# GpSimd makes o + 1 for both halves of an LSTM step, in place of ScalarE for the second half

## The chip, the cores and the metric

One core of one Trainium2 chip runs the whole program. The metric is the device time of one execution in microseconds (us); the figure for a kernel is the median of its runs. The engines are TensorE (PE; its weight loads are listed apart as PEld), VectorE (DVE), ScalarE (ACT), GpSimd (POOL) and SyncE (SP). Each runs its own list of instructions in order, and they wait for one another on semaphores.

## What is computed

Two layers with residuals over x of shape (8, 512, 512): batch 8, 512 time steps, width 512.

```python
def lstm_scan(x, h0, Wx, Wh, b):
    xW = jnp.einsum('ntd,dg->ntg', x, Wx) + b
    def step(carry, xw_t):
        prev_h, prev_c = carry
        a = xw_t + prev_h @ Wh
        i = sigmoid(a[:, :Hdim]);  f = sigmoid(a[:, Hdim:2*Hdim])
        o = sigmoid(a[:, 2*Hdim:3*Hdim]);  g = tanh(a[:, 3*Hdim:])
        next_c = f * prev_c + i * g
        next_h = o * jnp.tanh(next_c)
        return (next_h, next_c), next_h
x = x + lstm(x, cond, Wx, Wh, b)
x = x + ssm(x, cond, ...)   # a per-step filter, projections, a linear scan of 64 states, a projection
```

The LSTM's 512 steps depend on one another. The second layer follows block by block, 32 steps at a time, beside the steps of the first.

## The kernel before, in words

**Halves.** The 512 hidden units lie in four chunks of 128 partitions; half 0 of a step is chunks 0 and 1, half 1 is chunks 2 and 3. Each half has its own PSUM bank (recA, recB), its own buffers (`tr`, `pre`, `act`, `prod`, `tc`, `osc`, index 0 or 1) and its own semaphores. The recurrent product is made in fp16 with the weights as a high and a low part (`whi`, `wlo`) and the state as a high and a low part (`hb`), so the state of a half is ready only when both its parts are written.

**One step, engine by engine.** TensorE, `recur(t, half, k)` at L465, multiplies chunk k of the old state into one half's bank: 8 matmuls a call, in the order A0, A1, B0, A2, A3, B1, B2, B3 (letter: the bank; digit: k). A0 waits for both parts of the state's half 0 (`s_h[0]`), A2 for those of half 1 (`s_h[1]`). VectorE: `open_` (L812, transposes a bank to SBUF), `add` (L818, sums the high and low columns to `pre`), `product` (L823), `cell` (L828, the new c), `high` (L834, high part of h = osc * tc) and `low` (L840, low part, from GpSimd's h less the high part). ScalarE: `gates` (L699, one tanh for all four gates), `seeds` (L626, puts the next step's x part into a bank, ahead of time), `tanh_c` (L709, tc = tanh of c) and `opened` (L705). The sigmoids are made from tanh, so h needs (o + 1), scaled by SC = 4096; that is `osc`. `gates` puts the tanh of o in `act[q][:, 2, :]`; `osc[0]` is made from it by GpSimd (L400, a tensor_scalar on 128x16), `osc[1]` by ScalarE (L705). GpSimd then makes h = osc * tc in fp32 for each half (L406).

**What sets the order.** All of it is written out by hand, and an engine never leaves its order. ScalarE in step t:

```python
gates(t, 0); seeds(t + 1, 0); gates(t, 1); tanh_c(t, 0)
opened(t);   seeds(t + 1, 1); tanh_c(t, 1)
```

VectorE in step t: `open_(0), add(0), open_(1), product(0), add(1), cell(0), product(1), high(0), cell(1), low(0), high(1), low(1)`, and after every fourth step `output` (L849, adds h to the residual). GpSimd in step t: osc of half 0, h of half 0, h of half 1. Once a step's own instructions are issued, each of TensorE, ScalarE and VectorE does its `beside(t)`: a share of the projection of later x (L435), of the second layer's filter (L510), its softplus, scan and outputs, put on certain steps by planned costs (`post_at`, `project_at`). These jobs stand in the same queues as the steps.

Of the kernel before, what the change touches and what calls it, by code (L numbers as in the profile page):

```python
# [5 lines left out]
def lstm_ssm_kernel(nc: bass.Bass, x, cond, Wx, Wh, b, conv_b, Wp, bp, Ws, bs, A_log, dt_log, Wo, bo, out):  # L6
# [5 lines left out]
    ALU = mybir.AluOpType  # L12
    ACT = mybir.ActivationFunctionType
# [12 lines left out]
    SC = 4096.0  # L26
# [5 lines left out]
    with ctx:  # L32
        def sb(name, shape, dt=f32):
            return ctx.enter_context(nc.sbuf_tensor(name, shape, dt))
# [4 lines left out]
        def sem(name):  # L39
            return ctx.enter_context(nc.semaphore(name))  # L40
# [32 lines left out]
        scale = sb("scale", [128, 4])  # L73
        tr = [sb(f"tr{h}", [128, 2, G, 4, NB]) for h in range(2)]
        pre = [sb(f"pre{h}", [128, G, 2, NB]) for h in range(2)]
        act = [sb(f"act{h}", [128, G + 1, 2 * NB]) for h in range(2)]
        prod = [sb(f"prod{h}", [128, 2, 2 * NB]) for h in range(2)]
        tc = [sb(f"tc{h}", [128, 2 * NB]) for h in range(2)]
        osc = [sb(f"osc{h}", [128, 2 * NB]) for h in range(2)]
# [33 lines left out]
        s_os = [sem(f"s_os{q}") for q in range(2)]  # L113
# [22 lines left out]
        s_tg = [sem(f"s_tg{q}") for q in range(2)]  # L136
# [243 lines left out]
        @block.gpsimd  # L380
        def _(pool):
            pool.memset(ident[:, :], 0.0).then_inc(s_zero, 1)
            pool.wait_ge(s_zero, 1)
            pool.affine_select(out=ident[:, :], in_=ident[:, :], compare_op=ALU.not_equal, fill=1.0, base=0,
                               pattern=[[-1, 128]], channel_multiplier=1).then_inc(s_ident, 1)
            pool.memset(bhl[:, :].bitcast(f32), 0.0).then_inc(s_bz, 1)

            pool.wait_ge(s_bhi, 2)
            pool.tensor_tensor(bhl[32:33, :], brow[1], bhl[32:33, :].bitcast(f32), ALU.subtract).then_inc(s_bl, 1)
            for k in range(2, KC):  # L390

                if k == 2:
                    pool.wait_ge(s_bl, 1)
                else:
                    pool.wait_ge(s_wxl_p, k - 2)
                pool.wait_ge(s_wxh_a, k - 1)
                pool.tensor_tensor(wxl[:, k, :], rawx[k], wxh[:, k, :].bitcast(f32), ALU.subtract).then_inc(s_wxl_p, 1)
            for t in range(T):
                pool.wait_ge(s_tg[0], t + 1)
                pool.tensor_scalar(osc[0][:, :], act[0][:, 2, :], 1.0, SC, ALU.add, ALU.mult).then_inc(s_os[0], 1)  # L400
                for q in range(2):
                    pool.wait_ge(s_tc[q], t + 1)
                    pool.wait_ge(s_os[q], t + 1)
                    if t % HS == 0 and t and q == 0:
                        pool.wait_ge(s_yadd, t // HS)
                    pool.tensor_tensor(h32[:, 2 * q:2 * q + 2, t % HS, :],  # L406
                                       osc[q][:, :].rearrange("p (c b) -> p c b", c=2),
                                       tc[q][:, :].rearrange("p (c b) -> p c b", c=2), ALU.mult).then_inc(s_h32[q], 1)
# [183 lines left out]
        def _(act_eng):  # L592
# [29 lines left out]
            def seeds(t, q):  # L622

                if t % TS == 0 and q == 0:
                    act_eng.wait_ge(s_seedin[t // TS % 2], 256 * (t // TT + 1))
                act_eng.activation(rec[q][:, 0:256], seed[:, t // TS % 2, t % TS // 2, q, :],  # L626
                                   ACT.Copy, scale=mask[:, t % 2:t % 2 + 1]).then_inc(s_seed[q], 1)
# [50 lines left out]
            def beside(t):  # L678
                for i in range(NP):
                    order = post_order(i)  # L680
                    for j in range(len(order)):
                        if post_at[i][j] == t:
                            post(i, order[j])
                for j in due(t, *PAR, len(par_order)):
                    param(j)
                for n in range(NBLK):
                    for i in range(2):
                        if out_when[n, i][2] == t:
                            o_store(n, i)
                for g in range(2, NG):  # L690
                    for part in range(2):
                        if ev_when(g) + part == t:
                            x_evacuate(g, part)
                for g, c in tiles_done(t):
                    x_rows(g, c)

            def gates(t, q):
                act_eng.wait_ge(s_add[q], t + 1)
                act_eng.activation(act[q][:, 0:G, :].rearrange("p g n -> p (g n)"),  # L699
                                   pre[q][:, :, :, :].rearrange("p g c b -> p (g c b)"), ACT.Tanh, scale=gain).then_inc(s_tg[q], 1)  # L700

            def opened(t):

                act_eng.wait_ge(s_tg[1], t + 1)
                act_eng.activation(osc[1][:, :], act[1][:, 2, :], ACT.Copy, bias=SC, scale=SC).then_inc(s_os[1], 1)  # L705

            def tanh_c(t, q):
                act_eng.wait_ge(s_c[q], t + 2)
                act_eng.activation(tc[q][:, :], act[q][:, 4, :], ACT.Tanh, scale=0.5).then_inc(s_tc[q], 1)  # L709
# [44 lines left out]
            for t in range(END):  # L754
                if t < T:
                    gates(t, 0)
                    if t + 1 < T:
                        seeds(t + 1, 0)
                    gates(t, 1)
                    tanh_c(t, 0)  # L760
                    opened(t)
                    if t + 1 < T:
                        seeds(t + 1, 1)
                    tanh_c(t, 1)
                beside(t)
# [318 lines left out]
```

## Time and profile before

| | |
|---|---|
| median of 3 runs | 1992.09 us (1990.87 to 1992.61) |
| the profiled execution's own time | 1992.87 us |
| its span, first to last instruction | 1991.0 us |
| mean granted TensorE clock | 0.987 of full |
| busy: PE, PEld | 1791.8 us (90%), 1282.6 us (64%) |
| busy: VectorE | 1430.1 us (72%) |
| busy: ScalarE | 1043.9 us (52%) |
| busy: GpSimd | 349.4 us (18%) |
| steps run from / to | about 78 us to 1972 us |

Busy shares say how full an engine is, not which one sets the time: 512 steps hang on each other, and in each the work goes from engine to engine. Matmuls overlap, and their ends are modelled, so TensorE's busy time is not a measure of how near it is to its limit. Read the chain of waits and a single step first. Where a duration and a start are given below, the end is their sum; a start earlier than the previous end on the same engine means that the two overlap in the engine.

### The profile page before, as it was taken

The page shows a single profiled execution, that of the slowest core. Times are in us where ns is not written, and L with a number is a line of the kernel's source. Part 1 is how long each engine was busy: PE and PEld are TensorE (multiplying, and loading weights), DVE is VectorE, ACT ScalarE, POOL GpSimd, SP SyncE. Part 2 cuts the span into 40 slices and gives each one's busy share as a digit, 9 for nine tenths or more (in the row PEclk, how much of TensorE's full clock was granted, in tenths as well). Part 3 has the DMA queues.
Part 4 walks back from the last instruction along what each step waited for, and adds up shares of the span by engine and source line. Part 5 has one row for each costly group of instructions (what it writes and reads, how often), then busy time and mean ns, then how long its engine had stood idle before and what let it go on. Part 6 is the DMA issues. An engine that isn't in the chain of part 4 may idle for free.

```text
span 1991.0 us, 90455 instructions
## 1 busy us (share of the span) xinstructions
PE 1791.8 (90%) x36290; PEld 1282.6 (64%) x36290; DVE 1430.1 (72%) x6913; ACT 1043.9 (52%) x4056; POOL 349.4 (18%) x1546
## 2 busy tenths in 40 slices
PE   2688899999999999999999999999999999999976
PEld 1455666666666666666666666766666677666755
DVE  4577666777777777777767777777777777767775
ACT  3355555555555555555555555555555555555452
POOL 3011111111111111111111111111111111111110
PEclk8799999999999999999999999999999999999998
DMA  5111111111121111111111111111111111211100
GB/s 201 49 47 44 39 50 36 40 55 48 37 61 49 42 45 51 49 41 58 46 48 46 44 46 51 53 49 49 46 39 51 50 52 34 66 45 40 47 17 23
DMA packets 112284, 98.71 MB, mean 50 GB/s; under 512 B 20097, under 2 KB 86197, under 8 KB 110838
## 3 DMA queue, kind: packets, MB, share of 16 engines
q1 hardware_dynamic: 111490, 92.35, 15.3%
q8 instruction: 286, 4.69, 1.0%
q14 instruction: 134, 1.10, 0.2%
q10 hardware_dynamic: 374, 0.57, 0.1%
HBM read 50.90 MB, written 41.94 MB: 47 GB/s over the span
## 4 chain that ended last, share of the span: by engine, by line
PE 45%; DVE 33%; ACT 11%; issue 5%; POOL 4%; DMA 1%; SPq 0%; ACTq 0%; POOLq 0%; DVEq 0%
PE recA L465 25%; DVE tr L812 16%; PE recB L465 9%; DVE pre L818 7%; ACT act L699 5%; PE pw L435 5%; PE pbc L510 5%; POOL h L406 4%; DVE hb L840 3%; ACT tc L709 3%; DVE prod L823 2%; DMA xs<-in_L_cond_b_dram 1%; ACT recB L626 1%; DVE acc L893 1%; DVE st L914 0%
## 5 line engine op out<-in xcount | busy, mean ns | idle before, releaser
L699 ACT ACTIVATE act<-pre 128x64 f32<-128x64 f32 x1024 | 262.8, 257 | 874.0 <-DVE pre L818 857.6
L465 PE MATMUL recA<-whi,hb 128*16 128x256 f16 x8176 | 514.6, 274 | 137.8 <-DVE hb L840 131.3
L465 PE MATMUL recB<-wlo,hb 128*16 128x256 f16 x8176 | 513.2, 273 | 0.0
L465 PE MATMUL recB<-whi,hb 128*16 128x256 f16 x8176 | 513.2, 273 | 0.0
L465 PE MATMUL recA<-wlo,hb 128*16 128x256 f16 x8176 | 512.9, 273 | 0.0
L465 PEld LDWEIGHTS recA<-whi,hb 128*16 128x16 f16 x8176 | 200.0, 88 | 402.8 <-DVE hb L840 347.1
L812 DVE STREAM_TRANSPOSE tr<-recA 128x256 f32<-128x256 f32 x512 | 229.9, 449 | 215.5 <-PE recA L465 214.3
L510 PE MATMUL pbc<-yt,wpk 128*128 128x256 f32 (+5 forms) x1120 | 333.7, 402 | 0.0
L406 POOL TENSOR_TENSOR h<-osc,tc 128x16 f32<-128x16 f32 x1024 | 227.8, 222 | 500.8 <-ACT tc L709 500.8
L400 POOL TENSOR_SCALAR osc<-act 128x16 f32<-128x16 f32 x512 | 105.0, 205 | 1088.3 <-ACT act L699 1088.3
L823 DVE SCALAR_TENSOR_TENSOR prod<-act 128x32 f32<-128x32 f32 x1024 | 196.7, 192 | 126.4 <-ACT act L699 126.4
L818 DVE TENSOR_TENSOR pre<-tr 128x64 f32<-128x64 f32 x1024 | 229.3, 224 | 17.6
L626 ACT ACTIVATE recA<-seed,mask 128x256 f32<-128x256 f32 x512 | 236.1, 461 | 9.2 <-DMA seed<-xw_rows 9.2
L834 DVE TENSOR_TENSOR hb<-osc,tc 128x16 f16<-128x16 f32 x1024 | 178.1, 174 | 85.2 <-ACT tc L709 83.7
L626 ACT ACTIVATE recB<-seed,mask 128x256 f32<-128x256 f32 x512 | 236.1, 461 | 0.0
L435 PE MATMUL pw<-wxh,xh 128*128 128x512 f32 x504 | 228.0, 452 | 6.6 <-DVE wxl L785 5.8
L812 DVE STREAM_TRANSPOSE tr<-recB 128x256 f32<-128x256 f32 x512 | 230.0, 449 | 1.8 <-PE recB L465 1.8
L840 DVE TENSOR_TENSOR hb<-h,hb 128x16 f16<-128x16 f32 x1024 | 179.5, 175 | 70.8 <-POOL h L406 3.7
L510 PEld LDWEIGHTS pbc<-yt,wpk 128*128 128x128 f32 x1120 | 169.9, 190 | 90.6 <-issue 85.8
L435 PE MATMUL pw<-wxh,xl 128*128 128x512 f32 x504 | 219.6, 436 | 0.0
L465 PEld LDWEIGHTS recB<-wlo,hb 128*16 128x16 f16 x8176 | 204.7, 90 | 19.2
L465 PEld LDWEIGHTS recB<-whi,hb 128*16 128x16 f16 x8176 | 204.7, 90 | 19.1
(150 smaller groups left out, 2051.7 us busy)
## 6 DMA issues: line engine op xcount, KB each, us to landing
xw_rows<-xs SPq DMA_DIRECT2D x128, 256.0 KB, 2.1
seed<-xw_rows SPq DMA_DIRECT2D x1024, 32.0 KB, 1.9
out_dram<-ot SPq DMA_DIRECT2D x32, 256.0 KB, 3.0
xn<-in_x_dram SPq DMA_DIRECT2D x30, 256.0 KB
seed<-in_L_cond_Wh_dram SPq DMA_DIRECT2D x2, 1024.0 KB, 7.3
wpk<-in_L_cond_Wh_dram SPq DMA_DIRECT2D x2, 1024.0 KB, 14.7
wlo<-in_L_cond_Wx_dram SPq DMA_DIRECT2D x2, 1024.0 KB, 20.2
xs<-in_L_cond_Wx_dram SPq DMA_DIRECT2D x1, 1024.0 KB, 4.9
```

Of the source, the lines that this page charges most:

```text
L400: pool.tensor_scalar(osc[0][:, :], act[0][:, 2, :], 1.0, SC, ALU.add, ALU.mult).then_inc(s_os[0], 1)
L406: pool.tensor_tensor(h32[:, 2 * q:2 * q + 2, t % HS, :], osc[q][:, :].rearrange("p (c b) -> p c b", c=2), tc[q][:, :].rearrange("p (c b) - ...
L435: pe.matmul(out, xx[:, g % 2, k, :], wxm[w][:, k, c, :, :, :], start=(first and part == 0), stop=False)
L465: ins = pe.matmul(rec[half][32 * j:32 * j + 2 * NB, 0:256].rearrange("p (c f) -> p c f", c=2), h[:, k, :], w[:, k, :, :].rearrange("p (c j ...
L510: ins = pe.matmul(pbc[:, NB * (lo - a):NB * (hi - a)], wpk[:, k, c, :], yt[:, n % XR, c, NB * (lo + k):NB * (hi + k)], start=(j == 0), sto ...
L626: act_eng.activation(rec[q][:, 0:256], seed[:, t // TS % 2, t % TS // 2, q, :], ACT.Copy, scale=mask[:, t % 2:t % 2 + 1]).then_inc(s_seed[ ...
L699: act_eng.activation(act[q][:, 0:G, :].rearrange("p g n -> p (g n)"), pre[q][:, :, :, :].rearrange("p g c b -> p (g c b)"), ACT.Tanh, scal ...
L812: dve.transpose(tr[q][:, :, :, :, :].rearrange("p c g z b -> p (c g z b)"), rec[q][:, 0:256]).then_inc(s_tr[q], 1)
L818: dve.tensor_tensor(pre[q][:, :, :, :].rearrange("p g c b -> p c g b"), tr[q][:, :, :, 0, :], tr[q][:, :, :, 1, :], ALU.add).then_inc(s_ad ...
L823: dve.scalar_tensor_tensor(prod[q][:, :, :], act[q][:, 0:2, :], 1.0, act[q][:, 3:5, :], ALU.add, ALU.mult).then_inc(s_prod[q], 1)
L834: dve.tensor_tensor(hb[t % 2][:, 2 * q:2 * q + 2, 0:NB], osc[q][:, :].rearrange("p (c b) -> p c b", c=2), tc[q][:, :].rearrange("p (c b) - ...
L840: dve.tensor_tensor(hb[t % 2][:, 2 * q:2 * q + 2, NB:2 * NB], h32[:, 2 * q:2 * q + 2, t % HS, :], hb[t % 2][:, 2 * q:2 * q + 2, 0:NB], ALU ...
```

## The change

GpSimd makes `osc[1]` too, with the tensor_scalar that it uses for `osc[0]`, after h of half 0 and before h of half 1. ScalarE's `opened` is gone. The value is the same but for the order of add and multiply; nothing else is moved.

```diff
             for t in range(T):
-                pool.wait_ge(s_tg[0], t + 1)
-                pool.tensor_scalar(osc[0][:, :], act[0][:, 2, :], 1.0, SC, ALU.add, ALU.mult).then_inc(s_os[0], 1)
                 for q in range(2):
+
+                    pool.wait_ge(s_tg[q], t + 1)
+                    pool.tensor_scalar(osc[q][:, :], act[q][:, 2, :], 1.0, SC, ALU.add, ALU.mult).then_inc(s_os[q], 1)
                     pool.wait_ge(s_tc[q], t + 1)
                     pool.wait_ge(s_os[q], t + 1)
                     if t % HS == 0 and t and q == 0:
...
-
-            def opened(t):
-
-                act_eng.wait_ge(s_tg[1], t + 1)
-                act_eng.activation(osc[1][:, :], act[1][:, 2, :], ACT.Copy, bias=SC, scale=SC).then_inc(s_os[1], 1)
...
                     gates(t, 1)
                     tanh_c(t, 0)
-                    opened(t)
                     if t + 1 < T:
                         seeds(t + 1, 1)
                     tanh_c(t, 1)
```

## Rows read from the trace of the kernel before

**Rows 1.** The page: its span, and the chain that ended last by line.

```profile
span 1991.0 us, 90455 instructions
...
PE recA L465 25%; DVE tr L812 16%; PE recB L465 9%; DVE pre L818 7%; ACT act L699 5%; PE pw L435 5%; PE pbc L510 5%; POOL h L406 4%; DVE hb L840 3%; ACT tc L709 3%; DVE prod L823 2%; DMA xs<-in_L_cond_b_dram 1%; ACT recB L626 1%; DVE acc L893 1%; DVE st L914 0%
```

**Rows 2.** The chain in order of time from 1000 us: start, us, what.

```profile
1002.13 0.23 POOL h L406
...
1002.39 0.19 DVE hb L840
...
1002.62 0.61 PE recA L465 x16
```

**Rows 3.** All waits: engine line <- awaited: us in total, times, longest.

```profile
ACT act L699 <- DVE pre L818: 857.6, 500, 5.0
POOL h L406 <- ACT tc L709: 500.8, 1024, 1.9
...
DVE tr L812 <- PE recA L465: 214.3, 453, 13.1
...
DVE hb L840 <- POOL h L406: 3.7, 11, 0.5
```

**Rows 4.** ScalarE's timeline, one step: start, us, instruction [idle before <-releaser].

```profile
1001.69 0.26 ACT L699 ACTIVATE act<-pre 128x64 f32<-128x64 f32 x1
1001.85 0.20 ACT L709 ACTIVATE tc<-act 128x16 f32<-128x16 f32 x1
1001.98 0.22 ACT L705 ACTIVATE osc<-act 128x16 f32<-128x16 f32 x1
1002.10 0.46 ACT L626 ACTIVATE recB<-seed,mask 128x256 f32<-128x256 f32 x1
1002.50 0.20 ACT L709 ACTIVATE tc<-act 128x16 f32<-128x16 f32 x1
```

**Rows 5.** Timeline of VectorE, the same step.

```profile
1001.32 0.19 DVE L823 SCALAR_TENSOR_TENSOR prod<-act 128x32 f32<-128x32 f32 x1
1001.43 0.22 DVE L818 TENSOR_TENSOR pre<-tr 128x64 f32<-128x64 f32 x1
1001.57 0.16 DVE L828 SCALAR_TENSOR_TENSOR act<-prod 128x16 f32<-128x16 f32 x1
...
1002.20 0.18 DVE L828 SCALAR_TENSOR_TENSOR act<-prod 128x16 f32<-128x16 f32 x1
1002.39 0.17 DVE L840 TENSOR_TENSOR hb<-h,hb 128x16 f16<-128x16 f32 x1
1002.73 0.18 DVE L834 TENSOR_TENSOR hb<-osc,tc 128x16 f16<-128x16 f32 x1 [0.17 <-ACT tc L709]
1003.03 0.18 DVE L840 TENSOR_TENSOR hb<-h,hb 128x16 f16<-128x16 f32 x1
```

**Rows 6.** Timeline of GpSimd, the same step.

```profile
1001.38 0.20 POOL L400 TENSOR_SCALAR osc<-act 128x16 f32<-128x16 f32 x1 [2.02 <-ACT act L699]
1002.13 0.22 POOL L406 TENSOR_TENSOR h<-osc,tc 128x16 f32<-128x16 f32 x1 [0.55 <-ACT tc L709]
1002.77 0.22 POOL L406 TENSOR_TENSOR h<-osc,tc 128x16 f32<-128x16 f32 x1 [0.42 <-ACT tc L709]
```

**Rows 7.** Timeline of GpSimd at the program's start.

```profile
1.18 0.29 POOL L384 TENSOR_SCALAR_AFFINE_SELECT ident<-ident 128x128 f32<-128x128 f32 x1 [0.24 <-POOL ident L382]
1.41 1.81 POOL L386 MEMSET bhl<- 128x2048 f32 x1
```

**Rows 8.** Timeline of TensorE's weight loads, the step after.

```profile
1003.26 0.10 PEld L465 LDWEIGHTS recA<-whi,hb 128*16 128x16 f16 x4
```

**Rows 9.** Timeline of TensorE's matmuls, the same stretch.

```profile
1003.17 0.28 PE L465 MATMUL recB<-wlo,hb 128*16 128x256 f16 x4
1003.28 0.28 PE L465 MATMUL recA<-whi,hb 128*16 128x256 f16 x4
```

**Rows 10.** All instructions of line L823: duration ns min/median/max.

```profile
L823 DVE SCALAR_TENSOR_TENSOR prod<-act x1024: 149/192/195, 79.8 to 1970.9; 128x32 f32<-128x32 f32 x171
```

## The prediction

> **What bounds the kernel now.** I read the chain that ended last first [rows 1]. It is spread over all engines in short pieces: TensorE's bank A product, VectorE's transpose and sum, the gates, GpSimd's h, the low part of the state. That is a loop of dependent work, gone through 512 times, and no engine by itself. So busy shares are set aside, and the question is which instructions of a step lie on the loop.
>
> The chain in order of time answers it [rows 2]: it goes through GpSimd's h at 1002.13 us, the low part at 1002.39 and TensorE's first bank A product at 1002.62. Those are the instructions of **half 0**. VectorE's timeline has the same low part at 1002.39 and the one of half 1 only at 1003.03 [rows 5]. So the loop runs A0, ..., A3, transpose, sum, gates(0), product, cell, tanh_c(0), h of half 0, low of half 0, A0 again. The waits bear it out: VectorE waits 453 times for bank A's product, and ScalarE 500 times for the sum before gates [rows 3]. In most steps both are idle when the loop's work reaches them.
>
> Half 1 joins the loop at one place, A2, which needs low of half 1. That ends at 1003.03 + 0.18 = 1003.21, and the weight load of A2 starts 0.05 later, at 1003.26 [rows 5, 8]. Its matmul starts at 1003.28, just 0.11 after the one before it at 1003.17 [rows 9]; and from A0's start at 1002.62 it is six groups of 0.11, so TensorE has not stood still. Half 1 is in time, with at most 1003.28 - 1003.26 = 0.02 us to spare. This matters for both signs: **earlier half 1 gains nothing on the loop, later half 1 costs nearly its full lateness in each step.**
>
> **What the change removes.** ScalarE's osc[1] runs from 1001.98 to 1002.20. Behind it in the queue stand the seed of bank B at 1002.10 and tanh_c(1) at 1002.50 [rows 4]. tanh_c(0), which is on the loop, is ahead of it at 1001.85 and doesn't move. The seed starts 1002.10 - 1001.98 = 0.12 earlier, and so could tanh_c(1), at 1002.38. But it also needs cell(1), which ends at 1002.20 + 0.18 = 1002.38 [rows 5]. A hand-over from VectorE to ScalarE is 0.04: the sum of half 1 ends at 1001.43 + 0.22 = 1001.65, and gates(1) starts at 1001.69 [rows 4, 5]. So tanh_c(1) starts at 1002.42, 0.08 earlier than now, and ends at 1002.62. ScalarE's 512 x 0.22 = 113 us of work are gone, but it waits 858 us for VectorE already [rows 3], and that wait covers them: nothing on the loop.
>
> **What it adds.** GpSimd gets 512 tensor_scalars of 0.20 us [rows 6], 102 us, on an engine that waits 501 us for tc alone [rows 3]. The new one stands behind h of half 0, which ends at 1002.13 + 0.22 = 1002.35, and ahead of h of half 1, which starts at 1002.77: 0.42 of idle time [rows 6]. Its wait, for gates(1), was met at 1001.69 + 0.26 = 1001.95 [rows 4], before its turn, so nothing queues behind that wait. Queued behind the instruction are only h of half 1 and the next step, and no DMA. It needs 0.20 plus two gaps that no step shows now:
> - from h of half 0 to osc[1], with the wait already met. Lowest: at the program's start a memset follows with no wait of its own and starts at 1.41, where the instruction ahead ends at 1.18 + 0.29 = 1.47: -0.06 [rows 7]. Highest: 0.08, the hand-over from ScalarE to GpSimd (tc ends at 1001.85 + 0.20 = 1002.05, h starts at 1002.13 [rows 4, 6]). I take 0.00, near the memset, since this wait too is met.
> - from osc[1] to h of half 1, GpSimd waiting for itself. Lowest 0.04, the hand-over of GpSimd's h to VectorE (1002.35 to 1002.39 [rows 5, 6]); highest 0.24, the one such wait shown, at the start [rows 7]. I take 0.08, GpSimd's hand-over inside the loop, where the same instruction waits.
>
> So osc[1] ends at 1002.35 + 0.00 + 0.20 = 1002.55, and h of half 1 could start at 1002.63 for its sake. For tc it starts at 1002.62 + 0.08 = 1002.70. tc is later and decides: h of half 1 starts 0.07 earlier than its 1002.77. VectorE's high part of half 1 needs osc[1] and tc, and starts 0.03 behind tc as now [rows 4, 5], at 1002.65, after low of half 0 has ended at 1002.56. Then low of half 1 comes at 1002.96 instead of 1003.03, and A2's weights are loaded 0.07 earlier, ahead of a matmul that can't start before its turn at 1003.28. On the loop: **0**.
>
> **Where the 0.07 us does count.** The jobs beside the steps start when a step's last instructions are done. Where they end late, they would now end 0.07 earlier. On VectorE that can be at most the 512 - 453 = 59 steps in which it isn't seen waiting for bank A [rows 3]: between 0 and 59 x 0.07 = 4.1 us. I take a third, 1.4, since an instruction that ends just in time shows no idle time either, and gives nothing back. On ScalarE it is the 512 - 500 = 12 steps without a wait before gates(0): 0.8 us. Together -2.2 us.
>
> **Does it hinder what runs beside it?** osc[1] on GpSimd would lie at 1002.35 to 1002.55, over low of half 0 (1002.39 to 1002.56) on VectorE, which is on the loop. Bounds for the stretch: 0, because product(0) at 1001.32 runs under osc[0] at 1001.38, product(1) doesn't, and over all 1024 the median is 192 ns and the maximum 195 [rows 5, 6, 10]; or 0.02, because cell(1) at 1002.20, under h of half 0, is listed with 0.18 and cell(0) with 0.16 [rows 5]. I take 0: product is the row with the very GpSimd instruction that is added.
>
> The sum, against the profiled execution: 1992.87 - 2.2 = 1990.7, its span 1991.0 - 2.2 = 1988.8. The median of the runs shown is 0.8 lower than that execution, so 1992.09 - 2.2 = 1989.9; I say 1990.0. A measurement of this kernel can tell about 0.2%, 4 us, from no change.
>
> **Rivals.**
> 1. *GpSimd is late (slower).* The place is A2, the mechanism the two gaps. h of half 1 moves past today's start once the gaps sum to more than 0.42 - 0.20 = 0.22, and TensorE stands still once they pass 0.22 + 0.02 = 0.24. With both highest, 0.08 + 0.24 = 0.32, A2 is 0.08 late in the 453 steps in which bank A is waited for: 36 us, 2028. With 0.25 it is 0.01, 4.5 us, 1996.6. For it: the only wait of GpSimd for itself in the trace is 0.24. Against: that one is a different instruction in the program's first microseconds. Chance 0.08.
> 2. *A shared path (slower).* osc[1] stretches low of half 0. By cell's 0.02 it is 453 x 0.02 = 9 us, 2001; by half of that 4.5 us, 1996.6. The nearest row, product, speaks against it. Chance 0.07. The Trainium skill, GPSIMD Engine Reference, section Key points, says that GpSimd shares its SBUF interfaces with VectorE and contends with VectorE instructions that have two SBUF inputs. By that rule low of half 0, with its two, would be held up; product(0) has two SBUF inputs as well and shows nothing, so the trace doesn't bear it out.
> 3. *The steps with late jobs gain in full (faster).* 59 + 12 steps x 0.07 = 5.0 us, 1987.1. For it: VectorE is 72% busy, and where it shows no wait the queue may be full. Against: a stop that hides behind TensorE's own jobs in that step gives nothing back. Chance 0.18.
> That the change doesn't do what it says has no room here: osc[1] is made in one place, and one engine's instruction is gone.
>
> **How the numbers follow.** The forecast has 0.67, the rivals 0.08, 0.07 and 0.18. The range takes in the full gain of rival 3, 1987.1, down to 1986.8 for the spread of the runs, and the small ends of rivals 1 and 2, 1996.6, up to 1997.0. Left out are their large ends. Faster by over 0.2% is rival 3, 0.18; slower is rivals 1 and 2, 0.15; the rest, 0.67, is within 0.2%.
>
> **What would show it.** In the changed profile: 1024 tensor_scalars on GpSimd, none of osc on ScalarE; tanh_c(1) 0.08 earlier behind tanh_c(0), 0.57 instead of 0.65; osc[1] starting within 0.08 of h of half 0's end; idle time before h of half 1 with tc as its releaser, about 0.15; A2's weight load some 0.07 ahead of its matmul more than now; low of half 0 still at 0.17 to 0.18. I am wrong if h of half 1 starts later than 0.64 after h of half 0, if low of half 0 is longer or starts later, or if VectorE's wait for bank A grows.

## The result, and the profile after

The changed kernel takes 1995.22 us (median of 14 runs, 1994.06 to 2000.19) against 1992.15 for the kernel before on the same chips (14 runs): a ratio of 1.0018, 95% interval 1.001 to 1.0026. It is 3.1 us **slower**, where 2.2 us faster was forecast. The time lies inside the stated range and within the 0.2% that counts as no change; the sign is wrong. The profiled execution is the slowest of the 14, 2000.19 us, 5 us over the median; it is read here for what happens inside a step, and not for the total.

From the page of the changed kernel: its span, the busy times, the chain that ended last by line, and the two groups of GpSimd.

```profile
span 1998.4 us, 90455 instructions
...
PE 1796.5 (90%) x36290; PEld 1277.2 (64%) x36290; DVE 1429.4 (72%) x6913; ACT 1009.1 (50%) x3544; POOL 454.5 (23%) x2058
...
PE recA L466 24%; DVE tr L807 16%; PE recB L466 9%; DVE pre L813 7%; ACT act L700 5%; PE pw L436 5%; POOL h L407 5%; PE pbc L511 5%; DVE hb L835 3%; DVE prod L818 2%; ACT tc L705 2%; DMA xs<-in_L_cond_b_dram 1%; POOL osc L402 1%; DVE acc L888 1%; PE po L531 0%
...
L402 POOL TENSOR_SCALAR osc<-act 128x16 f32<-128x16 f32 x1024 | 209.8, 205 | 1125.5 <-ACT act L700 1082.5
...
L407 POOL TENSOR_TENSOR h<-osc,tc 128x16 f32<-128x16 f32 x1024 | 228.1, 223 | 364.1 <-ACT tc L705 287.2
```


GpSimd has its 1024 tensor_scalars (105 us more of work), ScalarE its 512 instructions less. In the chain GpSimd's h has gone from 4 to 5%, and osc, not in it before, has 1% [rows 1]: half 1 has got onto the chain in some of the steps.

The waits of the changed kernel, over the whole trace: engine line <- awaited: us in total, times, longest.

```profile
ACT act L700 <- DVE pre L813: 895.9, 500, 5.0
...
POOL h L407 <- ACT tc L705: 287.2, 520, 2.0
DVE tr L807 <- PE recA L466: 207.9, 449, 13.3
...
DVE hb L829 <- POOL osc L402: 92.9, 497, 0.6
...
DVE hb L835 <- POOL h L407: 7.6, 22, 0.5
```


GpSimd waits for tc 520 times instead of 1024 [rows 3]: in half 1 tc is no longer what h starts on. A new wait has come, VectorE's high part for GpSimd's osc, 497 times. And low waits for h as its own releaser 22 times instead of 11 [rows 3]; the eleven more turn out to be most of the steps that lose time.

One step of the changed kernel, GpSimd, then VectorE, then ScalarE (start us, us, instruction [idle before <-releaser]).

```profile
1004.77 0.22 POOL L407 TENSOR_TENSOR h<-osc,tc 128x16 f32<-128x16 f32 x1 [0.55 <-ACT tc L705]
1005.08 0.20 POOL L402 TENSOR_SCALAR osc<-act 128x16 f32<-128x16 f32 x1
1005.43 0.22 POOL L407 TENSOR_TENSOR h<-osc,tc 128x16 f32<-128x16 f32 x1
```

```profile
1005.03 0.18 DVE L835 TENSOR_TENSOR hb<-h,hb 128x16 f16<-128x16 f32 x1
1005.39 0.18 DVE L829 TENSOR_TENSOR hb<-osc,tc 128x16 f16<-128x16 f32 x1 [0.18 <-POOL osc L402]
1005.69 0.17 DVE L835 TENSOR_TENSOR hb<-h,hb 128x16 f16<-128x16 f32 x1
```

```profile
1004.49 0.20 ACT L705 ACTIVATE tc<-act 128x16 f32<-128x16 f32 x1
1004.60 0.46 ACT L627 ACTIVATE recB<-seed,mask 128x256 f32<-128x256 f32 x1
1005.06 0.21 ACT L705 ACTIVATE tc<-act 128x16 f32<-128x16 f32 x1
```


ScalarE does what was forecast: tanh_c(1) starts 1005.06 - 1004.49 = 0.57 behind tanh_c(0) instead of 0.65 [rows 4]. VectorE's low of half 0 still takes 0.18. But osc[1] starts 1005.08 - (1004.77 + 0.22) = 0.09 behind the end of h of half 0, and h of half 1 starts 1005.43 - (1005.08 + 0.20) = 0.15 behind the end of osc[1]. (To the nanosecond the medians over all steps are 0.084 and 0.148.) So h of half 1 is **0.66** behind h of half 0, where before it was 0.64 [rows 6] and 0.57 was forecast.

TensorE's matmuls of the next step in the changed kernel.

```profile
1005.26 0.29 PE L466 MATMUL recA<-whi,hb 128*16 128x256 f16 x4 [1.09 <-DVE hb L835]
...
1005.81 0.28 PE L466 MATMUL recB<-wlo,hb 128*16 128x256 f16 x4
1005.92 0.29 PE L466 MATMUL recA<-whi,hb 128*16 128x256 f16 x4
```


A2 comes 0.66 behind A0, in its turn, as before [rows 2, 9]. In the typical step the lateness of 0.02 is just about the spare time: the median from A0 to A2 is 0.659 in both traces. So where do 3 us come from? The matmuls' starts, summed over 511 steps of the two traces, say it: from A0 to A2 it is 339.1 us before and 342.7 after, 3.6 more. Only 15 steps are more than 0.02 longer than before, and they add 3.3 us. One step near the end is 0.58 shorter, which comes and goes between the traces of these runs whatever the change. The other 495 add 0.9 us, under 0.002 each.

### The profile page after: what moved, and what is told of

It reads as the page before. It is cut to its first block, busy times and chain, and to the rows that moved or that the text cites. A ratio compares the mean times of both kernels' runs of the same rounds, so it can differ in the third digit from the quotient of the medians.

```text
span 1998.4 us, 90455 instructions
## 1 busy us (share of the span) xinstructions
PE 1796.5 (90%) x36290; PEld 1277.2 (64%) x36290; DVE 1429.4 (72%) x6913; ACT 1009.1 (50%) x3544; POOL 454.5 (23%) x2058
## 4 chain that ended last, share of the span: by engine, by line
PE 45%; DVE 33%; ACT 10%; POOL 5%; issue 5%; DMA 1%; SPq 0%; ACTq 0%; POOLq 0%; DVEq 0%
PE recA L466 24%; DVE tr L807 16%; PE recB L466 9%; DVE pre L813 7%; ACT act L700 5%; PE pw L436 5%; POOL h L407 5%; PE pbc L511 5%; DVE hb L835 3%; DVE prod L818 2%; ACT tc L705 2%; DMA xs<-in_L_cond_b_dram 1%; POOL osc L402 1%; DVE acc L888 1%; PE po L531 0%
## 5 line engine op out<-in xcount | busy, mean ns | idle before, releaser
L402 POOL TENSOR_SCALAR osc<-act 128x16 f32<-128x16 f32 x1024 | 209.8, 205 | 1125.5 <-ACT act L700 1082.5
```

The source lines that it names most:

```text
L402: pool.tensor_scalar(osc[q][:, :], act[q][:, 2, :], 1.0, SC, ALU.add, ALU.mult).then_inc(s_os[q], 1)
```

## The experiments

The kernel before was timed again beside each group of runs, on the same chip. Each ratio is against those runs, with its 95% interval in brackets, and "us over" is the difference of the two medians. An interval is about 0.1% (2 us) wide to each side, so differences of 1 us between two experiments are read from the traces and not from the times. Steps are counted from 0, and sums over steps are each from the trace of one execution.

### Removal alone, addition alone

Nobody makes osc[1]; half 1 uses osc[0], on GpSimd as shown and on VectorE alike.

```diff
-                    opened(t)
...
-                                       osc[q][:, :].rearrange("p (c b) -> p c b", c=2),
+                                       osc[0][:, :].rearrange("p (c b) -> p c b", c=2),
```

> Nothing makes osc[1] any more, on either engine; h of half 1 is made with osc[0] (the values of half 1 are wrong, all waits but those on osc[1] stay). So this is the removal alone. Theory A (half 1 has become late: two gaps around osc[1] on GpSimd, 0.08 and 0.15 us, leave h of half 1 0.66 behind h of half 0 instead of 0.64): here h of half 1 is 0.56 behind, A2's matmul is 0.66 behind A0's, and the time is 1 to 3 us under the kernel before, 1989 to 1991. Theory B (it is not half 1's lateness but the removal that costs, by moving the seed of bank B and the jobs beside the steps): 1995, as after the change. Theory C (osc[1] on GpSimd disturbs its neighbours by running there): as A, 1989 to 1991.

Measured: 1991.6 against 1993.01, ratio 0.9988 (0.9979 to 0.9997). The waits of this run and GpSimd's step:

```profile
POOL h L406 <- ACT tc L704: 469.2, 1024, 1.9
...
DVE tr L806 <- PE recA L465: 245.9, 462, 13.3
```

```profile
1005.18 0.22 POOL L406 TENSOR_TENSOR h<-osc,tc 128x16 f32<-128x16 f32 x1 [0.55 <-ACT tc L704]
1005.76 0.22 POOL L406 TENSOR_TENSOR h<-osc,tc 128x16 f32<-128x16 f32 x1 [0.36 <-ACT tc L704]
```


The two h are 0.58 apart, as half 1's tc allows. VectorE waits 246 us for bank A instead of 214 [rows 3]: its queue is done 32 us earlier in all, and nearly all of it turns into waiting. The removal alone gains 1.4 us by the medians, 2.4 by the ratio (0.6 to 4.2 by its interval), where the forecast had 2.2. Theory B falls.

Now the kernel before, with a tensor_scalar on GpSimd that nobody needs.

```diff
                 for q in range(2):
+                    if q == 1:
+                        pool.wait_ge(s_tg[1], t + 1)
+                        pool.tensor_scalar(spare[:, :], act[1][:, 2, :], 1.0, SC, ALU.add, ALU.mult)
                     pool.wait_ge(s_tc[q], t + 1)
```

> The kernel before, ScalarE still making osc[1], with one more tensor_scalar of the same shape on GpSimd between its two products, which writes a spare buffer that nobody reads. Addition alone, without the dependence. Theory A: h of half 1 starts when tc is there, 0.64 behind h of half 0 as before, since the extra one ends 0.13 before and nobody waits for its result; time as before, 1991 to 1993. Theory C (GpSimd's instruction disturbs VectorE or the stalls of its own queue cost): about 1995, with low of half 0 longer than 0.175 or with more steps in which h of half 1 is late by 0.3 us.

Measured: 1993.34 against 1993.01, ratio 1.0002 (0.9993 to 1.0011). Low of half 0 keeps its 0.175 us (medians of before, after and this run). From A0 to A2 the trace has 339.3 us, against 339.1 before. So running something on GpSimd beside VectorE costs nothing that can be seen here; theory C falls, and with it rival 2.

### The loop and half 1's place in it

osc[1] ahead of h of half 0:

```diff
                 for q in range(2):
-
                     pool.wait_ge(s_tg[q], t + 1)
                     pool.tensor_scalar(osc[q][:, :], act[q][:, 2, :], 1.0, SC, ALU.add, ALU.mult).then_inc(s_os[q], 1)
+                for q in range(2):
                     pool.wait_ge(s_tc[q], t + 1)
```

> The changed kernel with GpSimd's osc[1] ahead of h of half 0 instead of behind it. gates(1) ends at about the time at which tanh_c(0) does less 0.10, so osc[1] would run right where h of half 0 is due. Theory A (the loop runs through half 0): h of half 0 starts 0.28 + about 0.2 to 0.3 behind tanh_c(0)'s start, the step grows by 0.2 to 0.28 us, and the time by 100 to 145 us, 2095 to 2140. If the loop had room in half 0: under 2000.

Measured: 2073.98 against 1993.01, +81 us, below the expected 95 to 145: h of half 0 came 0.465 behind tanh_c(0) instead of 0.281, so 0.18 late and not 0.2 to 0.3. 511 steps x 0.184 = 94 us, of which steps bound elsewhere swallowed some. Half 0 is on the loop.

One more tensor_scalar ahead of osc[1], for a dose of lateness in half 1:

```diff
                     pool.wait_ge(s_tg[q], t + 1)
+                    if q == 1:
+                        pool.tensor_scalar(spare[:, :], act[1][:, 2, :], 1.0, SC, ALU.add, ALU.mult)
                     pool.tensor_scalar(osc[q][:, :], ...
```

> The changed kernel with one more tensor_scalar of the same shape on GpSimd, into a spare buffer, ahead of osc[1]. A dose of lateness for half 1 alone. Theory A (half 1 is on the loop as soon as it is late): osc[1] starts 0.15 to 0.29 later behind h of half 0, h of half 1 is 0.81 to 0.95 behind, A2's matmul is late by nearly the same 0.14 to 0.28, and each step grows by that: 70 to 145 us over the kernel before. If half 1 had room beyond the 0.02: clearly less than that.

Measured: 2121.58 against 1992.74, +129 us, ratio 1.0645. The step on GpSimd:

```profile
1004.84 0.22 POOL L410 TENSOR_TENSOR h<-osc,tc 128x16 f32<-128x16 f32 x1 [0.55 <-ACT tc L708]
1005.14 0.20 POOL L404 TENSOR_SCALAR spare<-act 128x16 f32<-128x16 f32 x1
1005.40 0.20 POOL L405 TENSOR_SCALAR osc<-act 128x16 f32<-128x16 f32 x1
1005.76 0.22 POOL L410 TENSOR_TENSOR h<-osc,tc 128x16 f32<-128x16 f32 x1
```


The two h are 0.92 apart, 0.26 more than in the changed kernel, and the median step went from 3.65 to 3.92. From A0 to A2 the median is 0.924 instead of 0.659: 0.265 later, where h of half 1 is 0.28 later than before the change. So half 1 has about 0.02 us to spare and passes everything beyond it on, one for one.

### The order of two waits

In these traces an instruction with two waits gets the one written last as a bare wait of its own ahead of it; the first hangs on it. For half 1 they are swapped, on GpSimd and VectorE.

```diff
-                    pool.wait_ge(s_tc[q], t + 1)
-                    pool.wait_ge(s_os[q], t + 1)
+                    for s in ((s_tc, s_os) if q == 0 else (s_os, s_tc)):
+                        pool.wait_ge(s[q], t + 1)
...
-                dve.wait_ge(s_tc[q], t + 1)
-                dve.wait_ge(s_os[q], t + 1)
+                for s in ((s_tc, s_os) if q == 0 else (s_os, s_tc)):
+                    dve.wait_ge(s[q], t + 1)
```

> The changed kernel, with the order of the two waits ahead of h and of the high part swapped for half 1 (first osc, then tc), on GpSimd and VectorE. Then the wait for osc[1] hangs on the instruction itself, and the one for tc is an instruction of its own ahead of it. Theory A, with the part that the last wait to be met is the one ahead of the instruction: VectorE's high part of half 1 starts 0.03 to 0.04 behind osc[1]'s end instead of 0.10, h of half 1 starts 0.08 to 0.10 behind it instead of 0.15, so 0.61 behind h of half 0; A2 is in time again, and the time is 1990 to 1993. If the order of the waits has nothing to do with it (the result of a GpSimd tensor_scalar is just seen late): no change, 0.10 and 0.15, 1995. Theory C: 1995.

Measured: 1995.54 against 1993.01, ratio 1.0013 (1.0004 to 1.0022). GpSimd's step:

```profile
1006.61 0.22 POOL L407 TENSOR_TENSOR h<-osc,tc 128x16 f32<-128x16 f32 x1 [0.56 <-ACT tc L705]
1006.91 0.20 POOL L402 TENSOR_SCALAR osc<-act 128x16 f32<-128x16 f32 x1
1007.25 0.22 POOL L407 TENSOR_TENSOR h<-osc,tc 128x16 f32<-128x16 f32 x1
```


The two h are back at 0.64, but the gaps behind osc[1] shrank by only 0.014: from 0.148 to 0.134 on GpSimd, from 0.103 to 0.089 on VectorE. The median step is at 3.650 again as before the change (3.654 in the changed kernel), and yet the time is hardly better. With theory A's constant part undone, 2.5 us are still there. From A0 to A2 this trace has 342.8 us, and the whole excess of 3.7 is in 18 steps. The explanation by constant gaps was **not enough**. The swap also has a price of its own: in the eight steps in which ScalarE's tc of half 1 comes late, tc is now the bare wait, and h of half 1 is 0.93 behind instead of 0.87.

### Stops at fixed places of a list

The steps that lose time in the changed kernel have numbers. GpSimd in step 50, the changed kernel:

```profile
264.97 0.22 POOL L407 TENSOR_TENSOR h<-osc,tc 128x16 f32<-128x16 f32 x1 [0.55 <-ACT tc L705]
265.27 0.20 POOL L402 TENSOR_SCALAR osc<-act 128x16 f32<-128x16 f32 x1
265.92 0.22 POOL L407 TENSOR_TENSOR h<-osc,tc 128x16 f32<-128x16 f32 x1 [0.44 <-POOL osc L402]
```


osc[1] starts at its time, and then h of half 1 is 0.95 behind instead of 0.66, with 0.44 idle where tc had long been there. The same 0.29 is lost at steps 50, 114, 178, 242, 306, 370, 434 and 498, every 64 steps. Six of the eight reach A2, with 0.29 to 0.30 each, 1.8 us together. In the kernel before and in the one with the unneeded tensor_scalar there is no such stop at these steps (242 is late in them too, but with ScalarE's tc, as are seven other steps). The latter has the same number of GpSimd instructions, but its wait ahead of h, for ScalarE's osc[1], is met early. That made a theory D: GpSimd stops at fixed places of its instruction list; a stop hides where the engine waits anyway with its wait hanging on the next instruction, and shows where the wait ahead of it is met late.

The kernel before with both: the extra tensor_scalar, and h of half 1 waiting for it.

```diff
                 for q in range(2):
+                    if q == 1:
+                        pool.wait_ge(s_tg[1], t + 1)
+                        pool.tensor_scalar(spare[:, :], act[1][:, 2, :], 1.0, SC, ALU.add, ALU.mult).then_inc(s_spare, 1)
                     pool.wait_ge(s_tc[q], t + 1)
-                    pool.wait_ge(s_os[q], t + 1)
+                    pool.wait_ge(s_os[q] if q == 0 else s_spare, t + 1)
```

> The kernel before, ScalarE still making osc[1], with the extra tensor_scalar on GpSimd between its products into a spare buffer, and h of half 1 waiting for it (in place of osc[1], which is there earlier, as tc follows it on ScalarE). Unlike the run with the dummy that nobody waits for, this has GpSimd's wait for itself, and VectorE still gets osc[1] early. Theory A: h of half 1 is 0.66 behind h of half 0. Theory D with its reason (a stop at a fixed place in the list is hidden under a wait that hangs on the instruction behind it, and exposed behind a wait that stands ahead of it): the stops at steps 50, 114, ... return, while VectorE's four (94, 308, 315, 389) stay at 0.08. Time 2 to 3 us over the kernel before. If the stops come from the late osc[1] on VectorE or from something else of the removal: 0.64, no stops, the time of the kernel before.

Measured: 1995.39 against 1992.74, ratio 1.0012 (1.0003 to 1.0021). GpSimd in its step 50, and in the same step of the run with nobody waiting:

```profile
263.80 0.22 POOL L411 TENSOR_TENSOR h<-osc,tc 128x16 f32<-128x16 f32 x1 [0.55 <-ACT tc L714]
264.11 0.20 POOL L406 TENSOR_SCALAR spare<-act 128x16 f32<-128x16 f32 x1
264.76 0.22 POOL L411 TENSOR_TENSOR h<-osc,tc 128x16 f32<-128x16 f32 x1 [0.45 <-ACT tc L714]
```

```profile
262.31 0.22 POOL L410 TENSOR_TENSOR h<-osc,tc 128x16 f32<-128x16 f32 x1 [0.56 <-ACT tc L713]
262.61 0.20 POOL L405 TENSOR_SCALAR spare<-act 128x16 f32<-128x16 f32 x1
262.95 0.22 POOL L410 TENSOR_TENSOR h<-osc,tc 128x16 f32<-128x16 f32 x1
```


0.96 against 0.64. All eight stops are back and the median is 0.657. The only difference between these two kernels is whether h waits for the instruction ahead of it. GpSimd's **wait for itself** alone takes the ratio from 1.0002 to 1.0012; the intervals of the two overlap, but from A0 to A2 the traces have 339.3 us against 341.0, and 1.75 us stand in the six stops that reach A2. The releaser that the row names, ScalarE's tc, had been there long before.

Then the list was shifted against the stops.

```diff
+            for z in range(4):
+                pool.memset(spare[:, z:z + 1], 0.0)
             for t in range(T):
```

> The changed kernel, with four small memsets of a spare tile on GpSimd ahead of the first step. They cost nothing there; they move every later instruction of GpSimd's list by four places. Theory D (most of the loss is a stop of 0.29 us between osc[1] and h of half 1 that comes in GpSimd's list every 64 steps, at steps 50, 114, 178, ..., 498, since the place is fixed in the list): the stop now falls four instructions earlier in the list, behind osc[0], where GpSimd waits anyway; steps 50, 114, 178, 306, 370 and 434 are back at 0.66 between the two h, bank A's work from A0 to A2 loses about 1.7 us in all, and the time is 1.5 to 2 us under the changed kernel's. Theory A alone (only the constant gaps count): no change against the changed kernel, 1995.2.

Measured: 1996.29 against 1992.74, ratio 1.0018 (1.0009 to 1.0027). No gain. Steps 50, 114, ... are clean, but others stop now; GpSimd at step 92 of this run:

```profile
417.46 0.22 POOL L410 TENSOR_TENSOR h<-osc,tc 128x16 f32<-128x16 f32 x1 [0.56 <-ACT tc L708]
417.76 0.20 POOL L405 TENSOR_SCALAR osc<-act 128x16 f32<-128x16 f32 x1
418.41 0.22 POOL L410 TENSOR_TENSOR h<-osc,tc 128x16 f32<-128x16 f32 x1 [0.44 <-POOL osc L405]
```


The stops are at steps 28, 92, 156, ..., 476. So they do belong to places of the list: four memsets moved one set of eight away and another one in. With the waits swapped as well:

> Both: the waits of half 1 swapped and the four memsets ahead of the first step. Theories A and D together: the step in the middle is at 3.650 us as before the change, the 64-step stops are gone, and what is left are four steps (94, 308, 315, 389) in which VectorE's own stop of 0.29 is no longer hidden, about 1 us in all: 1 to 1.5 us over the kernel before. If D is wrong: as with the swapped waits alone, 2.5 us over the kernel before.

Measured: 1995.76 against 1992.74, ratio 1.0019 (1.001 to 1.0028), with the stops at 28, 92, ... too. Both expectations missed, and that gave the spacing. The trace records six GpSimd instructions a step, two of them bare waits. One stop every 128 instructions fits both numbers: 64 steps are 384 = 3 x 128 instructions, and from step 50 to step 92 it is 42 x 6 = 252 = 2 x 128 - 4. So the stops fall on three of the six places of a step in turn, every second one. In the run with the doubled tensor_scalar, seven a step, the stops come every 128 steps (61, 189, 317, 445), and 7 x 128 is again a multiple of 128. Numbered from 0 at the first GpSimd instruction that a trace records, the stopped h is number 68 of its 128 in every one of these stops: eight times each in the changed kernel, with the waits swapped, with GpSimd waiting for itself and with four memsets (with or without the swap), and four times with the doubled one. An odd shift moves all three to the other places:

```diff
+            for z in range(1):
+                pool.memset(spare[:, z:z + 1], 0.0)
```

> The changed kernel with one small memset on GpSimd ahead of the first step instead of four. With four, the stops of h of half 1 moved from steps 50, 114, ... to 28, 92, ..., still every 64 steps. GpSimd has six instructions a step (two tensor_scalars, two products, two waits of their own), so 64 steps are 384 = 3 x 128 of them. Theory D now with the spacing: there is a stop at every 128th instruction of GpSimd's list, at three of the six places of a step in turn; unshifted and with four those are the odd places, h of half 1 among them. One memset moves them to the even places: osc[0] and h of half 0 (both hidden, GpSimd has waited 0.3 us or more there) and the wait for osc[1] ahead of h of half 1. That last comes at steps 50, 114, ... and shows less, since the stop can begin while osc[1] is still being made: h of half 1 0.70 to 0.85 behind instead of 0.95. Time 0.5 to 1.5 us under the changed kernel. If the spacing is chance: stops of 0.29 at some other steps again, no change.

Measured: 1994.09 against 1991.9, ratio 1.0007 (0.9998 to 1.0016). GpSimd in step 50 of this run:

```profile
263.83 0.22 POOL L410 TENSOR_TENSOR h<-osc,tc 128x16 f32<-128x16 f32 x1 [0.55 <-ACT tc L708]
264.13 0.20 POOL L405 TENSOR_SCALAR osc<-act 128x16 f32<-128x16 f32 x1
264.49 0.22 POOL L410 TENSOR_TENSOR h<-osc,tc 128x16 f32<-128x16 f32 x1
```


0.66, where 0.70 to 0.85 was expected: the stop doesn't show at all. None is left at h of half 1 in any step but the eight that come with ScalarE's tc. Its excess over before from A0 to A2 is 1.9 us instead of 3.6 (3.7 with four memsets), so by the traces one memset took back about half of the loss. The times agree (2.2 us over instead of 3.1), but their intervals overlap and don't show it by themselves. With the waits swapped too:

> The same one memset, and the waits of half 1 swapped, so the best that the change can be made to do by its own means. Theories A and D: the median step at 3.650 us, no stop of 0.29 at h of half 1 but those that come with ScalarE's tc; left over against the kernel before are VectorE's stops that a late osc[1] exposes, about 1.5 us in all. 1 to 2 us over the kernel before; 0.5 to 1.5 under the run with four memsets and swapped waits.

Measured: 1994.76 against 1991.9, ratio 1.001 (1.0001 to 1.0019), 2.9 us over by the medians and 2.0 by the ratio, where 1 to 2 was expected. It is not told apart from the run above.

### What is left: VectorE's own stops

VectorE has such steps too. Step 94 in the kernel before, then in the changed one:

```profile
425.73 0.18 DVE L840 TENSOR_TENSOR hb<-h,hb 128x16 f16<-128x16 f32 x1
426.16 0.20 DVE L834 TENSOR_TENSOR hb<-osc,tc 128x16 f16<-128x16 f32 x1 [0.26 <-ACT tc L709]
```

```profile
426.78 0.18 DVE L835 TENSOR_TENSOR hb<-h,hb 128x16 f16<-128x16 f32 x1
427.49 0.17 DVE L829 TENSOR_TENSOR hb<-osc,tc 128x16 f16<-128x16 f32 x1 [0.54 <-POOL osc L402]
```


From low of half 0 to the high part of half 1 it is 0.43 before, 0.09 more than in the usual step [rows 5], and 0.71 after, 0.35 more. It is so in steps 94, 308, 315 and 389, with the waits swapped or not, and three more steps (109, 330, 447) lose 0.15 between high and low that weren't late before: about 1.5 us in all at A2. In the run in which only GpSimd waits for itself they are as before:

```profile
425.59 0.18 DVE L845 TENSOR_TENSOR hb<-h,hb 128x16 f16<-128x16 f32 x1
426.02 0.21 DVE L839 TENSOR_TENSOR hb<-osc,tc 128x16 f16<-128x16 f32 x1 [0.26 <-ACT tc L714]
```


426.02 - 425.59 = 0.43. So these belong to the late osc[1] on VectorE, and not to GpSimd.

That they are places of VectorE's list can be counted in the traces. In the kernel before, 13 times an instruction of half 1 (high or low) starts over 0.06 later than the median, and each of the 13 is number 63 or 64 of its 128, numbered in the same way. They make A2 late in 12 steps, 1.9 us, which the kernel paid all along. In the changed kernel there are 24: 16 at the same numbers, and 8 behind GpSimd's stops.

Last, VectorE makes osc[1] itself, between low of half 0 and the high part of half 1; GpSimd's second tensor_scalar is gone, and the waits of half 1 are swapped.

```diff
                     low(t, 0)
+                    opened(t)
                     high(t, 1)
```

> Neither ScalarE nor GpSimd: VectorE makes osc[1], a tensor_scalar between low of half 0 and the high part of half 1, where it is idle for 0.17 us now; the waits of half 1 with osc first, then tc. ScalarE and GpSimd are as in the run in which nobody makes osc[1]. Theory A: osc[1] ends about 1002.64 in the times of the step of the prediction, VectorE goes on with the high part 0.03 later, and h of half 1 starts for osc[1] 0.59 behind h of half 0, so earlier than the 0.64 of before: nothing late, GpSimd's list is no longer, and the time is between that of the run without osc[1] (1.4 us under) and the kernel before. If VectorE's extra work puts off the jobs beside the steps: up to 59 steps x 0.1 to 0.2 = 6 to 12 us over.

Measured: 1997.28 against 1991.9, ratio 1.0021 (1.0012 to 1.003). VectorE's step in this run:

```profile
1004.83 0.17 DVE L838 TENSOR_TENSOR hb<-h,hb 128x16 f16<-128x16 f32 x1
1004.92 0.17 DVE L827 TENSOR_SCALAR osc<-act 128x16 f32<-128x16 f32 x1
1005.17 0.18 DVE L832 TENSOR_TENSOR hb<-osc,tc 128x16 f16<-128x16 f32 x1
```

and GpSimd's h of both halves:

```profile
1004.57 0.22 POOL L406 TENSOR_TENSOR h<-osc,tc 128x16 f32<-128x16 f32 x1 [0.56 <-ACT tc L704]
1005.21 0.22 POOL L406 TENSOR_TENSOR h<-osc,tc 128x16 f32<-128x16 f32 x1 [0.42 <-DVE osc L827]
```


osc[1] ends at 1005.09; VectorE itself goes on 0.08 later, and h of half 1 starts at 1005.21, 0.12 later, so 0.64 behind h of half 0 and no earlier than before the change. VectorE's list is 512 instructions longer, so its stops fall in other steps. Of 31 late instructions of its half 1, 22 are at numbers 63 to 65 of 128; five come with ScalarE's tc, and four are behind GpSimd's own number 68, at steps 9, 137, 265 and 393 (five instructions a step, so again every 128 steps). A2 is late by over 0.02 us in 33 steps instead of 13: 7.4 us against 2.5. The expectation missed both. No version tried beats the kernel before; only the run that leaves osc[1] out does.

## Why the prediction was wrong, point by point

- **The loop: right.** Half 0 decides, half 1 has 0.02 us to spare and costs one for one beyond it. Both dose runs bear it out.
- **The removal: right, in mechanism and size.** tanh_c(1) came 0.08 earlier; ScalarE's 12 late steps gave 0.9 us in the changed kernel (13 steps by 0.07, summed from the traces), 0.8 in the forecast; the removal alone measured 1.4 to 2.4 us, 2.2 in the forecast.
- **The two gaps on GpSimd: the step that failed.** "I take 0.00, near the memset, since this wait too is met" measured 0.084, just over the upper bound of 0.08. "I take 0.08, GpSimd's hand-over inside the loop" measured 0.148, inside its bounds. Their sum was 0.08 in the forecast, 0.23 in the trace, and the point from which rival 1 decides was 0.22 for h and 0.24 for TensorE. So h of half 1 is 0.02 later than before and not 0.07 earlier, and VectorE's share of the forecast gain, 1.4 us, never came. The first choice leaned on the row that suited it, a memset in the program's first microseconds.
- **Rival 1 is what happened** in kind: late half 1, A2 as the place. That its small end, 1996.6 for a sum of 0.25, lies near the measured time is luck: the measured sum of 0.23 is below its own 0.24, and by its sum would have cost nothing. The price came mostly from a term that neither the forecast nor the rival had: stops at fixed places of GpSimd's and VectorE's lists, which a late wait uncovers. "Nothing queues behind that wait" looked only at osc[1]'s own wait; the wait that mattered stands behind it, h's for osc[1]. The doubling of the line "low <- h" from 11 to 22 is its trace in the profile: the eleven more are the eight stops of GpSimd and VectorE's steps 109, 330 and 447.
- **Rival 2 fell** in the run with an unneeded tensor_scalar. The rule of the Trainium skill, GPSIMD Engine Reference, section Key points, on contention with VectorE's two-input instructions is not borne out at this size: low of half 0 is 0.175 with osc[1] beside it or without.
- **Rival 3 is not borne out.** It had 5.0 us for an earlier half 1. The run without osc[1] has half 1 earlier (0.58) and gains 1.4 to 2.4 us, at most 4.2 by its interval. The change itself has half 1 later, so it couldn't reach it.

The loss, put together. The changed kernel's own trace is 5 us over its median, so the sum is made from the run with four memsets, which has the same ratio, 1.0018, and a trace of one of its faster executions. Its 511 steps take 3.4 us more than before: GpSimd's stops give 2.0 (seven of eight reach A2), VectorE's seven steps 1.5, and 14 earlier steps (13 of them ScalarE's) take back 1.0. The last 0.9 is spread thin, under 0.002 a step, and has no cause shown. The times of the runs bear out the signs but are too coarse for the parts: 1.0002 to 1.0012 for GpSimd's wait for itself, 0.9988 for the removal alone.

Open: why the result of a tensor_scalar is taken up 0.05 to 0.07 us later than that of the product (0.103 on VectorE where h is taken up in 0.034). The order of the waits explains 0.014 of it.

## What to carry to other kernels

Moving work to an idle engine is paid for in gaps, not in work: count a start gap and a wait for itself, here 0.08 and 0.15 us around 0.20 us of work, and compare the sum with the idle time of that place in one step. Here 0.08 + 0.20 + 0.15 against 0.42 was enough to be late. Where the idle time is used up, delays come to light that waiting had covered before, such as the stops in an engine's instruction list. Before believing a gain on one side of a chain, ask which half has no spare time, and measure the spare time from the next instruction's turn.

## What the runs showed of the hardware

- GpSimd's list has a stop of 0.29 us at every 128th instruction that the trace records, found by shifting the list by 4 and by 1 and by making it longer, and each at number 68 of 128. In these runs it shows at h of half 1 only where the bare wait ahead of h is met late; in the kernel before and with the unneeded tensor_scalar it doesn't. VectorE's list has its own, at numbers 63 to 65 of 128. That it is the loading of instructions is likely but not shown. The Trainium skill, Runtime: NRT & Kernel Launch, section Instruction fetch mechanics, says that instructions are refilled in blocks of 256 and that crossing a block is mostly hidden. The spacing here is half of that, counted in recorded instructions, and the uncovered stops of both engines are 3.5 us of what was lost in the run with four memsets.
- The same tensor_scalar on GpSimd does no harm that can be seen when nobody waits for it (1.0002), and costs about 2 us when the next instruction does (1.0012; from A0 to A2 the traces have 1.7 us between the two).
- ScalarE's tanh of half 1 takes 0.215 us instead of 0.199 in the traces in which osc[1] is gone from ScalarE (medians over all steps). There it starts at the end of the seed ahead of it (1005.06), where before it starts 0.06 ahead of that end [rows 4]. Whether that is the reason was not tested.
